# Products of zeros beside the real ones in layer one's weighted sum

## The reference, cut to what matters

```python
ex = jnp.exp(alpha - seg_max[edge_dst])
denom = jax.ops.segment_sum(ex, edge_dst, num_segments=N)
alpha = ex / (denom[edge_dst] + 1e-16)
attn = jax.ops.segment_sum(v * alpha[..., None], edge_dst, num_segments=N)
```

## Time and profile before

| | |
|---|---|
| time, median of three executions | 16084.6 us (16077.82, 16084.6, 16091.67) |
| the profiled execution's own time | 16079.79 us |
| its span in the profile | 16078.1 us |
| mean granted TensorE clock over the span | 0.69 |
| PE busy | 10302.2 us, 64% |
| PEld busy | 7980.5 us, 50% |
| DVE busy | 10167.2 us, 63% |
| ACT busy | 4495.2 us, 28% |
| POOL busy | 9058.1 us, 56% |

### The profile page before, as it was taken

One profiled execution on the slowest core, in us unless ns is written; L12 is line 12 of the kernel. 1 busy time (PEld: TensorE's weight loads), 2 busy tenths in 40 slices (PEclk: granted clock), 3 DMA queues, 4 the chain that ended last, 5 costly groups with the idle time before them and its releaser, 6 DMA issues. The chain is left out here.

```text
span 16078.1 us, 333902 instructions
## 1 busy us (share of the span) xinstructions
PE 10302.2 (64%) x72558; PEld 7980.5 (50%) x72559; DVE 10167.2 (63%) x36116; ACT 4495.2 (28%) x11901; POOL 9058.1 (56%) x10038
## 2 busy tenths in 40 slices
PE   6555555555537777767965656645566776667886
PEld 5333333333326666656853444422344664336886
DVE  9666666666643444437856777752365666887887
ACT  0111111111102333322113430025301223556886
POOL 0477777777745777767764445546400555554442
PEclk9777777777766777765556667755555665557998
DMA  9722222222242444453319997756653897885665
GB/s 369 303 80 79 81 81 79 79 83 79 79 94 58 80 80 80 80 79 71 68 28 279 324 309 223 224 163 218 191 176 89 279 278 257 270 267 204 212 212 160
DMA packets 2144346, 2589.93 MB, mean 161 GB/s; under 512 B 892242, under 2 KB 1761819, under 8 KB 2144195
## 3 DMA queue, kind: packets, MB, share of 16 engines
q1 hardware_dynamic: 1749158, 1741.66, 37.6%
q0 software_dynamic: 353792, 655.17, 13.1%
q10 hardware_dynamic: 41244, 191.56, 3.1%
HBM read 1738.44 MB, written 848.86 MB: 161 GB/s over the span
## 5 line engine op out<-in xcount | busy, mean ns | idle before, releaser
L566 POOL DMA_INDIRECT edges_by_dst<-rec,pos x1568 | 1541.2, 983 | 1029.1 <-DVE rec L501 555.5
L989 POOL DMA_INDIRECT sc_rows<-src_table,sc_idx x1664 | 1589.1, 955 | 607.9 <-issue 497.6
L566 POOL DMA_INDIRECT edges_by_cell<-rec,pos x1568 | 1545.5, 986 | 514.8 <-issue 497.4
L1756 PE MATMUL ex_rows<-table,ex_oh 128*128 x6528 | 1132.6, 339 | 884.8 <-DVE ex_stage L1732 335.7
L1844 PE MATMUL gs_part<-gs_rows,gs_oh 128*128 128x192 bf16 x6528 | 1024.4, 321 | 602.0 <-DVE gs_oh L1817 518.5
L1756 PEld LDWEIGHTS ex_rows<-table,ex_oh 128*128 128x128 bf16 x6528 | 724.9, 129 | 1292.3 <-issue 1252.6
L642 PE MATMUL xps<-ident,ea 128*128 128x128 f32 x784 | 216.4, 431 | 1740.9 <-DMA ea<-in_edge_attr_dram 1740.9
L1844 PEld LDWEIGHTS gs_part<-gs_rows,gs_oh 128*128 128x128 bf16 x6528 | 697.0, 131 | 929.3 <-issue 613.5
L2224 ACT ACTIVATE key_in_block<-at_rows,first_node 128x66 f32<-128x66 f32 x4352 | 1083.3, 336 | 266.2 <-PE at_part L2252 244.9
L2252 PE MATMUL at_part<-cell_edge_term,key_in_block 128*66 128x128 f32 x8704 | 1062.7, 286 | 115.3 <-issue 96.4
L530 DVE SCALAR_TENSOR_TENSOR junk<-rowb,keycol,earlier 128x128 f32<-128x128 f32 (+1 forms) x3136 | 1124.5, 415 | 1.8
(11 more groups left out here) (402 smaller groups left out, 27327.5 us busy)
## 6 DMA issues: line engine op xcount, KB each, us to landing
ex_keys<-src_key_rows SPq DMA_DIRECT2D x1632, 128.0 KB
gs_rows<-dst_rows_by_src SPq DMA_DIRECT2D x1088, 192.0 KB
rowb<-sort_key_rows SPq DMA_DIRECT2D x392, 512.0 KB, 5.2
ex_keys<-dst_key_rows SPq DMA_DIRECT2D x1088, 128.0 KB
dst_rows_by_src<-patY ACTq DMA_DIRECT2D x1, 104448.0 KB, 417.2
rows_by_src<-ex_stage SPq DMA_DIRECT2D x544, 192.0 KB
scored_dst_rows_by_src<-patZ ACTq DMA_DIRECT2D x1, 71808.0 KB, 637.9
scored_rows_by_src<-ex_stage SPq DMA_DIRECT2D x544, 132.0 KB
```

Of the source, the lines that this page charges most:

```text
L566: nc.gpsimd.indirect_dma_start(out=out, out_offset=bass.IndirectOffsetOnAxis(ap=pos[:, u, k, j:j + 1], axis=0), in_=row, in_offset=None).t ...
L989: nc.gpsimd.indirect_dma_start(out=rows[:, u, j, :], out_offset=None, in_=tabS, in_offset=bass.IndirectOffsetOnAxis(ap=idx[:, u, j:j + 1], ...
L1756: m = nc.tensor.matmul(rows[k][u % 2][r // 2][:, r % 2, 0:W], oh[k][:, u % 2, r * P:(r + 1) * P], t3[:, bass.ds(held[k][u], 1), :].rearran ...
```

## The change

A new helper `occupy` does a number of products of zeros by zeros in bfloat16, as wide as the bank that it is given. The stage gets one more PSUM bank, `idle`, of 512 float32 columns, which nothing reads. TensorE does 24 such products as the stage begins, before its first wait, and one behind the four real products of each group, after the semaphore of the group has been raised.

```diff
+def occupy(nc, K, bank, times):
+
+    w = bank.shape[1] // P
+    for _ in range(times):
+        nc.tensor.matmul(bank[:, :], K.zero[:, :], bcast(K.zero[:, :], 1, [P, w, P]), start=True, stop=True)
+
+
 def node_stage(nc, counts, D, K, name, kin, weights, widths, feed, evict, table=None, bias=True, carrier=None, carried=0):
...
         part = [ctx.enter_context(nc.psum_tensor(f"{name}_part{u}", [P, G, P], F32)) for u in range(RING)]
+        idle = ctx.enter_context(nc.psum_tensor(f"{name}_idle", [P, 4 * P], F32))
...
                         for j in range(G):
                             m = nc.tensor.matmul(part[u][:, j, 0:width], oh[:, u, j, :], msg[:, u, j, 0:width], start=True, stop=True)
                         m.then_inc(s_mm.sem, 1)
+                        occupy(nc, K, idle, 1)
+                occupy(nc, K, idle, 24)
                 loop(pe, n, body)
```

## The result

| | before | after |
|---|---|---|
| time, median of 20 executions | 16080.51 us (16071.06 to 16091.67) | 16111.14 us (16104.94 to 16118.13) |
| the profiled execution | 16079.79 us | 16116.69 us |
| its span | 16078.1 us | 16115.0 us |
| mean granted clock over the span | 0.690 | 0.687 |
| first product of the stage to VectorE's final add | 819.9 us | 850.1 us |

The ratio is 1.0019, with a 95% interval of 1.0012 to 1.0026: slower by a fifth of a per cent, which is small but clear of the noise. The forecast was 16136 us and slower; the direction is right, and the size is 25 us too large. The medians lie 30.6 us apart and the stage grew by 30.2 us, so it holds the whole difference. (The two profiled executions lie 36.9 us apart; the 6.7 us of that outside the stage are less than the 13 to 21 us over which the executions of one kernel spread.)

The account below looks back on a forecast made before the run. GpSimd was taken to bound the stage at about 7.8 us a pass, TensorE close under. 104 x 8.33 plus 4.2 is 870.5 against 819.9, +50.6; with 3 for stalls +54, so 16136 us, range 16098 to 16180.

Parts of the forecast that it names:

- The bound before, and the one after: In the stage: GpSimd binds before at about 7.8 us a pass; with the change TensorE does, at 8.33 us.
- The clock stays at 0.50: In the stage's loop: one product of zeros a group leaves TensorE's granted clock at its lower level, 1.2 GHz.
- The price of one product of zeros: In the loop: each of 416 products adds 0.164 + 0.42 - 0.214 = 0.37 us (0.32 to 0.42).
- The load of weights: On TensorE: the skill's rule would leave loads in the open, 0.53 us a product, some 115 us later; rejected.
- The stalls: In passes with a third scatter, 8.74 us against TensorE's 8.33: only 3 us added (0 to 8).
- The end: From the stage's last product to VectorE's final add: 4.2 us, with GpSimd no longer lagging by a pass.
- The last step of the sum: Whole kernel: 16079.8 + 54 = 16134, then 16136 since the median shown is 4.8 us over the profiled time.
- The 24: Products of zeros before the loop: cost nothing, 10 us if uncovered; clock rises, then falls before the first real group.
- Rival 1: In the loop: the clock comes up and GpSimd's own time binds, -25 us, 16055; chance 0.10.
- Rivals 2 and 3: In the loop: zeros stand in the open, +140 us, 16220, chance 0.04; pauses stay, 154 us, 16234, chance 0.03.

## Why the prediction was right, and where its size was off

- **The bound before, and the one after.** Right. GpSimd set the stage (774 us when it had 120 scatters fewer), with TensorE close under it; with the change TensorE does (848 us, scatters or not). The waits changed sides as forecast: 585 to 5 us for ScalarE on GpSimd, 0.5 us a pass for GpSimd on the sums (48.1 / 104).
- **The clock stays at 0.50.** Right, over 850 us, though TensorE is busy 99.5% of them. The Trainium skill ("TensorE: Matmul & The Clock Gate", Part 1, "What's actually happening") has the clock released by how busy the array has been; taken as the busy time of a profile, this stage contradicts it. The grounds were weaker than the call. The 73% for the stage at 0.78 counts 0.16 us for each product also where the clock was high, and can't be: TensorE was busy 514 of those 800 us, 64%, and 68% in the stage at 0.52. And the run that rose has narrower weights as well (128x66 against 128x128), so the moving side is not shown to be the difference. That one product a group stays low while two rise could not be read from these rows; in that the call was partly lucky.
- **The price of one product of zeros.** This is the term of the sum that was mis-sized. I took 0.164 us for the step from a float32 record to the zeros, the middle of 0.114 and 0.214, on the ground that a record's load of weights doesn't shrink with its columns. Measured: 1.60 - 7 x 0.213 = 0.11 us, the lower end, in the changed kernel and at half width alike. That is 68/128 of the 0.214 us seen behind 128 columns, so the load of the zeros' weights adds nothing there; why two float32 records stay 0.213 us apart whatever their columns, no run takes apart. That makes 0.32 us a product and 8.13 us a pass instead of 0.37 and 8.33: 104 x 0.20 = 21 of the 24 us by which the stage's forecast (819.9 + 54) was over the 850.1 measured.
- **The load of weights.** The runs side with the earlier trace rows: 0.43 us for 512 columns and 0.22 for 256, loads included, with all products on the whole array. The Trainium skill (same page, Part 3, "The mechanism") has the sentence that the prediction set against the rows, a load overlaps a product only in another row group; the runs contradict it. The same section also lets a load into a background buffer of weights go ahead of running products; the prediction left that out, and it would fit the runs.
- **The stalls.** I added 3 us for passes with a third scatter. There are none: TensorE idles less than 4 us in all, and these lie behind its last product. This is the other part of the 24 us.
- **The end.** 4.2 us forecast; 4.5 measured behind the start of the last zeros, 4.0 behind their 0.43 us.
- **The last step of the sum.** 16079.8 + 54 + 4.8 is 16139, not 16136; and over 20 executions the median before is 16080.5, so the 4.8 us were not there to add.
- **The 24.** Right in what they cost: alone they leave the stage at 821 us and the ratio at 1.0001 (0.9987 to 1.0016), and the clock fell before the first message, as the earlier trace rows had it. The times were off: they started at 7332.6, not 7335, the clock rose after 3 us instead of six, and the short rise lay between 7335 and 7343 instead of 7338 and 7346.
- **Rival 1, the clock rises.** Not with one product a group. Its price was wrong as well: with four a group and the clock at 0.98 the stage is 829 us, not the 795 that -25 gives. That a seventh of the stage at the high clock suffices for no loss was not put to a test: no kernel had so small a share (823 to 830 us at 0.82 to 0.98).
- **Rivals 2 and 3.** Neither: the zeros add 0.32 us each, and the pauses were absorbed.

## What to carry to other kernels

Work added to an engine that is nearly level with the bound costs what reaches past the bound, not its sum: 416 x 0.32 = 133 us were added here, and 30 of them seen. So work out the pace of each engine a pass (6.85, 7.8 and 6.3 us for TensorE, GpSimd and VectorE here) and compare the new one with the highest. Products of zeros are worth trying only when they raise the clock and waits for products hold the stage; read those waits first, since the same four a group were worth nothing behind GpSimd's bound, 34 us with it relieved, and 70 us where VectorE and TensorE waited for each other. And read the whole time too: in none of these kernels did it get shorter.

## What was not expected of the hardware

- Two products of zeros a group raise the clock without help from the start, and it then goes up and down (0.82 and 0.85 on average), while one a group leaves it at 0.50 even when it begins high. A group at the low clock takes 2.03 us with one and 2.46 with two, without a pause in either: a small difference with a sharp effect.
- A product whose weights change from float32 to bfloat16 behind 68 moving columns follows after 0.11 us, half the step between two float32 records (0.213).
- With four zeros a group GpSimd's own busy time was 599.7 us, against 588.1 with none in the loop, in kernels whose GpSimd code is the same, and that stage is 8 us longer. Its adds took 416 ns each on average instead of 404. It needs no zeros: with 120 scatters fewer and no products of zeros they took 441 ns. What slows GpSimd is open, and so is whether it is the cause of the 8 us.
